# One block without stops for a four-stage masked, low-rank and routed layer stack

## The reference

```python
x = _layernorm(x + _L0_attn_ref(x, weight, mask))   # A: x @ (W0 where its 32x32 block's mask sum > 0).T
x = _layernorm(x + _L0_ffn_ref(x, ...))             # B: x @ W1.T + bias + low-rank adapter of the batch
x = _layernorm(x + _L1_attn_ref(x, ...))            # M, C: small model of width 128, see below
x = _layernorm(x + _L1_ffn_ref(x, ...))             # D: x @ W3.T + bias + sum over 8 experts of routed low rank
```

## Time and profile before

| | us |
|---|---|
| median of three runs | 1999.91 (1998.6, 1999.91, 2013.88) |
| the profiled execution | 2012.65 |
| its span, mean granted PE clock | 2010.9, 0.918 |
| PE busy | 1827.5 (91%) |
| DVE, ACT, POOL busy | 1030.3, 631.4, 538.4 |
| setup | 0 to 60 |
| A | 60 to 426 |
| first parts of B, B | 426 to 507, 507 to 983 |
| passage to M, M, its last turns | 983 to 1055, 1055 to 1318, 1318 to 1358 |
| C, router and first parts of D | 1358 to 1550, 1550 to 1602 |
| D, from its last product to the end | 1602 to 2004, 7 |

### The profile page before, as it was taken

The page is one execution under the profiler, slowest core; times in us unless marked ns, Lnnn a source line. Parts: engine busy times, 40 slices in busy tenths (PEclk is TensorE's granted clock), DMA queues, the critical chain, the costliest instruction groups (busy, mean ns, idle before and its releaser), DMA issues. The chain is left out here.

```text
span 2010.9 us, 25961 instructions
## 1 busy us (share of the span) xinstructions
PE 1827.5 (91%) x8103; PEld 1408.7 (70%) x8103; DVE 1030.3 (51%) x1877; ACT 631.4 (31%) x900; POOL 538.4 (27%) x681
## 2 busy tenths in 40 slices
PE   1899999968999999999659999998996799999998
PEld 0688788855787878788547766664553588878887
DVE  5356422235555455543246777745865555555542
ACT  1232333333223232322125555542322323232221
POOL 3011111123000000000068988932543300000000
PEclk9999999977999999999859999995755899999999
DMA  4322262223322223222140000004753433333321
GB/s 178 129 84 84 105 245 86 104 94 120 106 103 100 103 101 103 100 84 79 45 165 1 1 1 1 1 1 170 241 197 136 133 126 130 136 123 118 129 93 65
DMA packets 78796, 207.28 MB, mean 103 GB/s; under 512 B 10041, under 2 KB 23609, under 8 KB 77772
## 3 DMA queue, kind: packets, MB, share of 16 engines
q1 hardware_dynamic: 57580, 135.96, 20.2%
q10 hardware_dynamic: 21088, 69.74, 8.6%
HBM read 129.24 MB, written 76.42 MB: 102 GB/s over the span
## 5 line engine op out<-in xcount | busy, mean ns | idle before, releaser
L259 PE MATMUL A_ps_out<-wall,A_x_hi 128*128 128x512 f32 x512 | 201.9, 394 | 12.2 <-DVE A_x_lo L501 8.8
L259 PE MATMUL B_ps_out<-wall,B_x_hi 128*128 128x512 f32 x512 | 207.3, 405 | 0.0
L259 PE MATMUL D_ps_out<-wall_d,D_x_hi 128*128 128x512 f32 x512 | 204.0, 398 | 0.0
L260 PE MATMUL B_ps_out<-wall,B_x_hi 128*128 128x512 f32 x512 | 201.6, 394 | 0.0
L261 PE MATMUL B_ps_out<-wall,B_x_lo 128*128 128x512 f32 x512 | 201.6, 394 | 0.0
L260 PE MATMUL D_ps_out<-wall_d,D_x_hi 128*128 128x512 f32 x512 | 201.3, 393 | 0.0
L261 PE MATMUL D_ps_out<-wall_d,D_x_lo 128*128 128x512 f32 x512 | 201.2, 393 | 0.0
L260 PE MATMUL A_ps_out<-wall,A_x_hi 128*128 128x512 f32 x512 | 201.0, 393 | 0.0
L261 PE MATMUL A_ps_out<-wall,A_x_lo 128*128 128x512 f32 x512 | 200.9, 392 | 0.0
L566 DVE BATCH_NORM_STATS2 A_stats<-A_row 128x6 f32<-128x512 f32 x64 | 44.4, 694 | 198.9 <-ACT A_row L411 197.5
L643 POOL TENSOR_SCALAR B_var_eps<-B_mean_var 128x1 f32<-128x1 f32 x32 | 6.1, 190 | 465.2 <-DVE B_mean_var L574 465.2
(11 more groups left out here) (282 smaller groups left out, 3667.0 us busy)
## 6 DMA issues: line engine op xcount, KB each, us to landing
A_x_in<-in_x_t SPq DMA_DIRECT2D x32, 512.0 KB, 3.4
x_scratch<-A_row ACTq DMA_DIRECT2D x32, 512.0 KB, 2.6
B_x_in<-x_scratch SPq DMA_DIRECT2D x32, 512.0 KB, 3.9
x_scratch<-B_row ACTq DMA_DIRECT2D x32, 512.0 KB, 2.6
C_x_in<-x_scratch SPq DMA_DIRECT2D x32, 512.0 KB, 4.0
x_scratch<-C_row ACTq DMA_DIRECT2D x32, 512.0 KB, 3.4
D_x_in<-x_scratch SPq DMA_DIRECT2D x32, 512.0 KB, 4.2
out<-D_row ACTq DMA_DIRECT2D x32, 512.0 KB, 2.6
```

The lines of the kernel that those rows point to most:

```text
L259: pe.matmul(ps_out[h][:], x_hi[:, s, k], walls[par][:, 0, k, cols], start=(k == 0), stop=False)
L260: pe.matmul(ps_out[h][:], x_hi[:, s, k], walls[par][:, 1, k, cols], start=False, stop=False)
```

## The change

All phases become one `build` with one `nc.Block`. Nothing is looped; every engine's program is written out for all 96 dense tiles (s = 0 to 95), 41 turns of M and the readout. What it does in detail:

- SBUF tensors get fixed offsets in regions shared by stage (`at`, `small`). Two walls, `wall_x` and `wall_y`, serve A, the four batches of B and the four of D in turn. x stays split in two places, PSUM is one tensor of eight banks.
- W0: the first three tiles of x are loaded and split early; PE multiplies chunk k of W0 for these three tiles (six banks) as soon as it is built, behind spreading chunk k+2.
- The 16 parts of B's first batch are built beside A's last 16 tiles, one to a tile. A's products alternate over two pairs of banks.
- The table is computed beside the last batch of B and stays in SBUF, as do the MLP weights; bias rows are made in turns 2 and 3 of M.
- The last layernorm becomes eight further steps of M (32 to 39, letters a and b only); z goes split to DRAM, or for batch 0 straight into the readout, in turns 34 to 38.
- The readout's bias is added to x before: beside M, SP loads each tile of x2, DVE adds `c_bias` and SP stores it back (`add_shared`).
- D: per batch, the 16 parts are built just ahead of their use by the first two tiles (the "pair"), the second tile four parts behind the first. The low half of odd parts is written on POOL. Beside the other six tiles the readout of the next batch and its router run. There is no building two to a tile any more.

```diff
+    wall_x = at("wall_x", X, [P, KC, 2, D], F32R)
+    wall_y = at("wall_y", Y, [P, KC, 2, D], F32R)
+    walls = [wall_y, wall_x, wall_y, wall_x, wall_x, wall_y, wall_x, wall_y]
...
+            def load_part(n):                                        # SP
+                b, k, o, _ = part_place(n)
...
+                at_least(sp, a_hi_ready, n - 1)
+                at_least(sp, a_lo_ready, n - 1)
+                sp.dma_start(a_in[:rank, n % 2], a_from[:, k * P:(k + 1) * P]).then_inc(a_loaded[n % 2], 16)
+                if n >= 2:
+                    sp.wait_ge(w_hi_ready, n - 1)
+                    low_parts(sp, n - 2)
+                sp.dma_start(w_in[:, n % 2], w_from[k][:, o * HALF:(o + 1) * HALF]).then_inc(w_loaded[n % 2], 16)
...
+            load_shared(0)
+            for i in range(TILES):
+                if i + 1 < TILES:
+                    load_shared(i + 1)
+                store_shared(i)
...
+            for b in range(BATCHES):
+                p, n, c = B_END + TPB * b, PARTS * (BATCHES + b), TPB * (b + 1)
+                for i in range(2, PARTS):
+                    load_part(n + i)
+                    if i == 6:
+                        load_c(c)
+                        load_z(c)
+                    if i == 8:
+                        load_x(p + 2)
+                    if i == 10:
+                        load_c(c + 1)
+                        load_z(c + 1)
+                    if i == 12:
+                        load_c(c + 2)
...
+            for k in range(2):                                       # PE, the start
+                spread_blocks(k)
+            for k in range(KC):
+                if k + 2 < KC:
+                    spread_blocks(k + 2)
+                first_products(k)
...
+            for b in range(BATCHES):                                 # PE, stage D
+                p, n, c = B_END + TPB * b, PARTS * (BATCHES + b), TPB * (b + 1)
+                for i in range(2):
+                    weight_part(n + i)
+                if b == 0:
+                    turn_x(p + 1)
+                for i in range(PARTS + LAG):
+                    if i + 2 < PARTS:
+                        weight_part(n + i + 2)
+                    if i < PARTS:
+                        pair_part(p, i)
+                    if i >= LAG:
+                        pair_part(p + 1, i - LAG)
+                    if i == 10:
+                        turn_x(p + 2)
+                for s in range(p + 2, p + TPB):
+                    j, more = s % TPB, b + 1 < BATCHES
+                    tiles = [c + i for i in C_STEP.get(j, ())] if more else []
+                    if s + 1 < D_END:
+                        turn_x(s + 1)
+                    if tiles:
+                        read_out(tiles[0])
+                    product(s, 0)
+                    if tiles:
+                        read_out(tiles[1])
...
+                for i in range(PARTS):                               # ACT, in a pair
+                    if i + 2 < PARTS:
+                        split_a(n + i + 2)
+                    weight_hi(n + i)
...
+            block_sums(0)                                            # DVE, the start
+            for k in range(KC + 2):
+                if k + 1 < KC:
+                    block_sums(k + 1)
+                if k < KC:
+                    compare(k)
+                if 1 <= k <= KC:
+                    add_identity(k - 1)
+                if k >= 2:
+                    w0_low(k - 2)
...
+            def add_shared(i, half):                                 # DVE, beside M, behind add_hidden
+                cols = slice(half * HALF, (half + 1) * HALF)
...
+                dve.tensor_tensor(shared[i % 2][:, cols], shared[i % 2][:, cols], c_bias[:, cols], ALU.add)\
+                   .then_inc(shared_added, 1)
...
+                for i in range(PARTS):                               # DVE, in a pair
+                    weight_sum(n + i)
+                    if i + 2 < PARTS:
+                        split_a(n + i + 2)
+                    if i % 2 == 0:
+                        weight_lo(n + i)
```

More of the change, by code:

```diff
@@ L31 @@
 AX = mybir.AxisListType.X
[L34 to L46, removed]
-    with ExitStack() as ctx:
[L48 to L52, removed]
-        def sem(name):
[L55 to L173, removed]
@@ new lines, in x_slot, with before_in_slot, out_bank, part_place @@
+def x_slot(s):
+    return s if s < FIRST else (s - FIRST) % 2
+def before_in_slot(s):
+    return s - FIRST if s < FIRST + 2 else s - 2
+def out_bank(s, h):
+    if s < FIRST:
+        return 2 * s + h
+    if s < A_END:
+        return 2 * ((s - FIRST) % 2) + h
+    return 5 + h if in_pair(s) and s % TPB == 1 else h
+def part_place(n):
+    u = n % PARTS
+    k, o = u % KC, u // KC
+    return n // PARTS, k, o, o == k * P // HALF
+def diagonals(n):
+    return sum(part_place(i)[3] for i in range(n + 1))
@@ new lines, in product @@
+            def product(s, half, chunks=range(KC)):
+                if chunks[0] == 0:
+                    if half == 0:
+                        pe.wait_ge(hi_ready, s + 1)
+                        pe.wait_ge(lo_ready, s + 1)
+                    bank_free(s, half)
+                if A_END <= s < B_END and s % TPB == 0:
+                    n = PARTS * batch_of(s) + KC * (half + 1)
+                    pe.wait_ge(w_hi_ready, n)
+                    low_parts(pe, n - 1)
+                wall = wall_x if s < A_END else walls[batch_of(s)]
+                for k in chunks:
+                    last = terms(s, half, k, wall)
+                if chunks[-1] == KC - 1:
+                    last.then_inc(mm_done, 1)
@@ new lines, in router_exp @@
+            def router_exp(batch):
+                act.wait_ge(shifted, batch + 1)
+                act.activation(chance[:], logits[:], ACT.Exp).then_inc(exp_done, 1)
+            w0_hi(0)
+            split_x(0)
+            w0_hi(1)
+            split_x(1)
+            split_x(2)
+            for k in range(2, KC):
+                w0_hi(k)
+            evacuate(0, 0)
+            split_x(FIRST)
+            evacuate(0, 1)
+            evacuate(1, 0)
+            evacuate(1, 1)
+            normalise(0)
@@ new lines, in _ @@
+            for s in range(A_END, B_END):
+                b, j, i = batch_of(s), s % TPB, s - A_END
+                n = PARTS * (b + 1) + 2 * j
+                more = b + 1 < BATCHES
+                if s + 1 < B_END:
+                    split_x(s + 1)
+                if more:
+                    split_a(n)
+                    if j == 0:
+                        split_b(b + 1)
+                    split_a(n + 1)
+                normalise(s - 1)
+                if more:
+                    weight_hi(n)
+                if i % 2 and i >= 3:
+                    evacuate_h((i - 3) // 2)
+                if more:
+                    weight_hi(n + 1)
+                if i >= 1:
+                    split_y(s - 1)
```

2827 lines of the change are left out of this document (1436 added, 1391 removed).

## The result

The changed kernel takes 2120.98 us (2118.26 to 2122.53, four runs), the kernel before 2002.26 (1998.6 to 2013.88, four runs). The ratio is 1.058 (95% interval 1.0535 to 1.0627). Forecast was 2048, +48 us; measured is +119. Of the 73 us between 2048 and 2121, 61 lie in the sum (2059 forecast, 2120.4 measured as span, so that spans rose by 109.5 where the sum had 48) and 12 in the base: I took off 13 us because the profiled run of before lay as much above its median, and the profiled run of after (2122.09) lies only 1 above its own.

A forecast was written before the change was run, and what follows sets the result against it. PE was taken to bound the dense stages and M, with POOL nearly a second bound there. Terms 412 + 508.5 + 463 + 668 + 7.5 gave a span of 2059, taken as 2048 us; range 1970 to 2125.

The forecast's parts named there:

- the start: First weights beside three tiles: compares wait behind products, chunk steps of 6.4 to 10.3 us, done at 79 us.
- the adds: Bias adds beside M: DVE adds and POOL's rotations exclude each other in SBUF, costing 46 us; 14 if only DVE's time counts.
- the pairs: First two tiles of each batch in D: building parts at 4.9 us each makes 85 us a pair, four times 340.
- the tail of M: Turns 33 to 40 with the readout of batch 0, up to D's first part: 98 us.
- near nothing: In B, the removed loop stop and the added bias matmuls and table work, about 5 us each, cancel; 508.5 us.
- the ring a, split, high half, low half, w, a: In D's pairs, SP's queue, a's landing, ACT's steps and the low half wait on each other: mean 4.9 us a part.
- rival 1: Faster: if a loads run ahead in D, PE's work sets the pairs, 45 us instead of 85; 1888 us, 14%.
- the passage to M: From B's last product to turn 6 of M: 56 us, against 72 before.
- the six tiles behind them: Rest of each batch in D: 83.8 us in three batches with two readouts in four tiles, PE staying the bound.
- the clock behind a pair: In D, a fourfold slow start of the clock after the pairs: 6 us.
- The forecast's own range: Span of times given to the main forecast of 2048 us, held at 52%: 2010 to 2095 us.
- rival 3: Much slower: pair steps 0.8 us longer, M at +2.6 a turn, first products at half clock; 2136 us, 11%.

The follow-up runs named there:

- e1: Changed kernel with the load of a for part n+1 issued ahead of the load of w for part n in the pairs: 2003.99 us.
- e9: Changed kernel with four places for w in D instead of two, SP's order left as it was: 1960.99 us, ratio 0.975 to the kernel before.
- e2: Changed kernel with the readout's bias row kept in PSUM, so DVE's adds beside M read it there instead of from SBUF: 2084.38 us.
- e6: Changed kernel with, in M's last turns, ACT's next squares ahead of normalising and the first of two tiles moved into the turn: 2106.99 us.
- e4: Changed kernel with the table and MLP weights made in 16 small pieces, two to a tile, beside B's last batch: 2102.11 us.
- e3: Changed kernel with W0's block sums spread four chunks ahead of the products instead of two, in PSUM columns of their own: 2104.52 us.

## Why the prediction missed, step by step

The direction was right, and the chains named for the start, the adds and the pairs came as described. What failed is the size of other terms: the tail of M (98 for 114.8), "near nothing" for B (508.5 for 520.9), and smaller sums of the same sign, 61 us in all, and then 12 for the base. The steps behind the first two are that ACT's place in a turn was taken as free, and that DVE's work beside B was compared as a sum.

- **The pairs: right.** 85 us forecast, 86.8 in the middle two, and 79.9 in the last, which has no loads of a readout between and a step of 5.0 us, for the 4.9 forecast; the ring a, split, high half, low half, w, a was named, and e1 and e9 show it by breaking it. The point from which it decides (2.5 us a part) and the price beyond it (45 us a pair) were put in rival 1; e9 gives 45.4. Rival 1 was right as a conditional, and needed an edit that the change did not have.
- **The adds beside M: right.** 46 us were forecast for turns 6 to 32, 50 came (313.4 for 263). e2 takes 40 of them back; the 10 that stay are what I take for DVE's own time, where I had put 14.
- **The tail of M: too small, 98 for 115.** The largest miss of a single term. I summed DVE's passes and took ACT's place in the turn as free. What the runs show in its place is that ACT does the next unit's squares behind two normalisations, so the readout's chain and the turn's stand one behind the other, at half the clock. e6, which moves these squares ahead and one of two tiles into the turn, takes 17 us off this stretch.
- **B: too small, 508.5 for 520.9.** "Near nothing", with 10 as the most, was the step that failed by its reasoning: I compared DVE's sum of work with the time and not where in a tile the lump falls. The last batch lost 22 us against before, the other three made up for some of it. e4 gives back 19.
- **The rest: D 12 us too small, the passage to M 7, A 5, the start 4, turns 6 to 32 4.** In D, 6 are in the pairs and 12 in the six tiles behind them (87.9 for 83.8, three times, with PE busy for nearly all of it), less the 6 that I had added for the clock behind a pair, which no run shows: the row of six tiles has the full clock throughout. All errors have the same sign. Each stretch was costed by its longest chain with no term for what else falls in, and seven such sums in a row do not average out.
- **The step of the start: mechanism right.** Steps of 6.4 to 10.3 us were forecast, 10.1, 9.6, 7.9, 9.5 and 9.5 came; e3, with the spreads two chunks further ahead, has none of the 3.45 us waits.
- **The range's upper end**, 2125, held the time by 4 us. The forecast's own range, 2010 to 2095, did not; the measured time is nearest to rival 3 (2136), but of its three parts (longer steps in the pairs, 2.6 us a turn, half the clock in the first products) none came in full. That the time is inside the stated range at all is due to the width left for rival 3.

## What to carry to other kernels

When a small load and a large one share an in-order queue, ask of each for which earlier part it waits through its neighbour, and not only through its own place. Counting the parts between that wait and the use tells what to expect: here 5.5, 3.1 and 2.3 us a part with 1, 2 or 3 parts in a round, and two more places of 2 KB a partition turned 5.8% slower into 2.5% faster. A stop that is taken away is worth what takes its place: each stretch looked at here had filled with a new chain, and each gave way to a small edit, of an order in e1, e3, e4 and e6, of a number of places in e9, of an operand's place in e2.

An engine that is busy for 60% of a stretch has no room unless the room is where the work is put.

## What the runs showed of the hardware that I had not expected

- Of two DVE adds of 512 beside POOL's rotations, both operands in SBUF, one waits and the other does not: of the 64 adds the shortest took 0.68 us, as did the median, and the longest 1.80. With one operand in PSUM all 64 took 0.68. The rotation that they meet (`y_rot`) fell from a median of 1.72 to 1.28 us with it, so the cost of the meeting is paid on both sides.
- The granted clock followed the gaps: 0.74 in a pair of 87 us, 0.91 at 57 us, 0.96 at 45.5, with the same matmuls. PE's busy time fell with it, from 55.0 to 43.8 and 38.3 us.
- A pair moves the same 8 MB in each of these three, at 92, 141 and 176 GB/s, so 92 was no limit of the path. In e1 a load of a still reached ACT 2.5 us after its issue (1594.34 to 1596.83).
